# Second layer of a two-layer network: slots find their tokens by an on-chip table instead of a scattered copy

## The reference

```
xn = layernorm(x)
q, k, v = split(xn @ w_qkv);  p = softmax(q k^T / sqrt(128)) per head
attn = (p v) @ w_out
score = relu(xn @ rw1 + rb1) @ rw2 + rb2;  gate = softmax(score over the top 2)
ffn = sum_e gate_e * (relu(xn @ W1[e] + b1[e]) @ W2[e] + b2[e])
x = x + attn + ffn
```

## Time and profile before

| | |
|---|---|
| median of 3 runs | 1158.14 us |
| lowest, highest | 1155.06, 1163.66 us |
| profiled execution | span 1215.3 us, first to last instruction; no other time of it is given |
| mean granted TensorE clock in it | 0.927 of full speed |
| busy in it: PE, DVE, ACT, POOL | 83%, 74%, 65%, 46% |
| weight loads of PE | 45% (beside PE) |

### The profile page before, as it was taken

How to read it: one execution, slowest core, us unless ns; L and a number is a source line. 1 busy time by engine, 2 the same in 40 slices (tenths; PEclk the granted TensorE clock), 3 DMA queues, 4 the chain that set the end, 5 groups by cost and what they waited for, 6 DMA issues and landing times. The chain is left out here.

```text
span 1215.3 us, 24799 instructions
## 1 busy us (share of the span) xinstructions
PE 1012.9 (83%) x9866; PEld 549.0 (45%) x9866; DVE 894.8 (74%) x1046; ACT 790.0 (65%) x851; POOL 563.5 (46%) x569
## 2 busy tenths in 40 slices
PE   6778777889888988888877779986899999998558
PEld 4522222334775333333337776344345656555123
DVE  7888888996648999999959356773685775667137
ACT  3699999998646999999976214311466566554244
POOL 5198887376655588888863005077000000000720
PEclk9799999999699999999997989986799999898679
DMA  8840101120872222222119800002023444321100
GB/s 301 241 160 31 33 33 33 36 69 30 241 159 63 63 72 71 69 70 72 52 43 275 195 2 22 1 25 93 22 79 112 123 124 137 87 79 47 51 25 26
DMA packets 117419, 105.32 MB, mean 87 GB/s; under 512 B 11862, under 2 KB 103666, under 8 KB 116658
## 3 DMA queue, kind: packets, MB, share of 16 engines
q1 hardware_dynamic: 107220, 83.41, 24.1%
q0 software_dynamic: 8512, 20.13, 5.7%
q10 hardware_dynamic: 1571, 0.20, 0.1%
HBM read 62.16 MB, written 38.39 MB: 83 GB/s over the span
## 5 line engine op out<-in xcount | busy, mean ns | idle before, releaser
L261 DVE SCALAR_TENSOR_TENSOR ring<-AD,PT 128x1808 f32<-128x1808 f32 (+15 forms) x128 | 282.9, 2225 | 27.1 <-issue 13.3
L976 PE MATMUL LG<-ring,lred 128*32 128x456 f32 (+15 forms) x2048 | 232.5, 573 | 0.0
L2259 ACT ACTIVATE EX<-SS 128x1024 f32<-128x1024 f32 x128 | 130.8, 1030 | 125.9 <-PE SS L2046 61.8
L2329 DVE TENSOR_REDUCE MX<-SS 128x2 f32<-128x1024 f32 x119 | 144.7, 1219 | 71.1 <-PE SS L2046 52.3
L267 POOL DMA_INDIRECT ys<-rows,goali x80 | 162.2, 2028 | 64.1 <-DVE rows L860 40.5
L916 ACT ACTIVATE ring<-ring 128x3680 f32<-128x3680 f32 (+15 forms) x47 | 161.2, 3430 | 3.6 <-DVE ring L261 3.6
L1001 PE MATMUL SD<-DSf,eyes 99*32 99x456 bf16 (+15 forms) x1280 | 95.2, 374 | 77.6 <-ACT ring L921 66.6
L769 POOL DMA_INDIRECT xs<-rows,sloti x64 | 134.4, 2099 | 30.7 <-issue 19.2
L922 ACT ACTIVATE ring<-ring 128x1824 f32<-128x1824 f32 (+15 forms) x80 | 145.9, 1823 | 0.0
L1963 POOL DMA_INDIRECT XN<-ys,sloti x16 | 16.4, 1024 | 271.7 <-PE SS L2056 267.1
L261 DVE SCALAR_TENSOR_TENSOR ring<-AD,bdmg 128x1808 f32<-128x1808 f32 (+15 forms) x48 | 106.5, 2219 | 0.0
(11 more groups left out here) (419 smaller groups left out, 1767.8 us busy)
## 6 DMA issues: line engine op xcount, KB each, us to landing
w1s<-in_L_ffn_W SPq DMA_DIRECT2D x39, 256.0 KB
w2s<-in_L_ffn_W SPq DMA_DIRECT2D x39, 256.0 KB
band<-ring SPq DMA_DIRECT2D x6, 1024.0 KB, 6.5
xl<-xs SPq DMA_DIRECT2D x20, 272.0 KB, 3.1
xs<-Z SPq DMA_DIRECT2D x5, 1024.0 KB, 8.9
w1s<-w1d SPq DMA_DIRECT2D x80, 64.0 KB
w2s<-w2d SPq DMA_DIRECT2D x80, 64.0 KB
band<-Z SPq DMA_DIRECT2D x4, 1024.0 KB, 9.7
```

The costliest lines, as they stand in the source:

```text
L261: return v.scalar_tensor_tensor(out=tile[:, s, :, t0:T], in0=AD[:, s, :, j + t0:j + T], scalar=extra, in1=AD[:, s, :, PAD + t0:PAD + T], o ...
L976: mm = pe.matmul(LG[32 * b:32 * b + 32, par, s, t0:T], lred[:, s, n % 4, :], ring[:, slot, s, b, t0:T], start=(n % 4 == 0), stop=(n % 4 == 3))
L2259: act.activation(EX[:, Q % 2, hh:hh + 2, t, :], SS[:, slot, :, :], ACT.Exp, scale=SCALE1).then_inc(freed[slot], 1)
L2329: v.tensor_reduce(MX[:, t, p // 2, hh:hh + 2], pairs_of(b, name), AX.X, ALU.max).then_inc(freed[slot], 1)
```

## The change

The array xs goes, with its zeroing and both scatters. XN is stored as it is to xnd in DRAM (one plain DMA of SP). Instead of each pair sending its row to its slot, each slot looks up its token. The table for that is made on chip: DVE compares the pairs' slots with the edges of the 40 tiles (reached_edges, at step 31 of stage 0) and the slots within a tile with the 128 lanes (lanes_of_pairs, four times); POOL makes from the first a mask of pair and tile, and that mask times the token's tile and place (tiles_of_pairs); 32 bf16 products of TensorE (sort_pairs, at step 2 of stage 1) contract both over the pairs into 128 x 120 numbers: for each slot the token's tile, its place, and whether it is a second choice. DVE turns these into row numbers (tokens_of_slots): toki, the token of a slot, and goali, the row of ys for its output. POOL then gathers the rows of xnd for a group of four tiles with four indirect DMAs (gather) and sends the group's outputs with as many indirect scatters to ys (store), where they now stand in the order of the tokens; empty slots go to rows of their own behind. At the end eight plain loads of SP bring them back in place of the 32 gathers. SP's queue keeps the weights, now in a plain loop. The experts start at step 10 of stage 1 instead of 19, and the fillers of steps 3 and 4 there are left out.

The diff, cut to its core:

```diff
@@ -41,8 +41,12 @@
 ROWS = 4 * GROUPS * P
+PAIRS1 = B * T * K1
 AHEAD = 3
-START_STEP = 19
+START_STEP = 10
+SLOT_STEP = 31
+LANE_STEPS = ((0, 32), (0, 33), (0, 35), (1, 0))
+TABLE_STEP = 2
 EPS = 1e-5
@@ -226,8 +230,6 @@
-    xs = nc.dram_tensor("xs", [ROWS, C], F32, kind="Internal").ap()
-    carried[-1].append(xs)
@@ -718,10 +720,6 @@
-                    flat = xs.rearrange("(p n) c -> p (n c)", p=P)
-                    span = GROUPS * 4 * C // 4
-                    for i in range(4):
-                        sp.dma_start(flat[:, span * i:span * i + span], zeros.rearrange("p q t -> p (q t)")[:, 0:span]).then_inc(d_zero, 16)
@@ -927,7 +925,7 @@
-                        act.wait_ge(d_zero, 128)
+                        act.wait_ge(d_zero, 64)
@@ -1453,8 +1451,9 @@
-    attT, wcp, route, b2r, d_zero, (xs,) = carried
-    ys = nc.dram_tensor("ys", [ROWS, C], F32, kind="Internal").ap()
+    attT, wcp, route, b2r, d_zero = carried
+    xnd = nc.dram_tensor("xnd", [B * T, C], F32, kind="Internal").ap()
+    ys = nc.dram_tensor("ys", [PAIRS1 + ROWS, C], F32, kind="Internal").ap()
@@ -1529,6 +1535,8 @@
+            sp.wait_ge(xn_ready, B)
+            sp.dma_start(xnd.rearrange("(n p) c -> p n c", p=P), XN[:]).then_inc(d_w[2], 16)
@@ -1654,6 +1667,12 @@
+    NM = ROWS // P
+    reached = w1s[:].rearrange("p a f -> p (a f)")[:, 0:K1 * TT * (NM + 1)].rearrange("p (n m) -> p n m", m=NM + 1)
+    in_lane = XN[:].rearrange("p t c -> p (t c)").bitcast(BF16).rearrange("p (n r) -> p n r", r=P)
+    in_tile = [buf[:].rearrange("p a n c -> p (a n c)").bitcast(BF16)[:, 0:TT * 3 * NM].rearrange("p (t w m) -> p t w m", t=TT, w=3)
+               for buf in (xl, xsT)]
@@ -1662,6 +1681,7 @@
+    PT1 = PYy[:, 1, 0:3 * NM]
@@ -1824,15 +1845,6 @@
-        def load(n):
-            if n >= 2:
-                sp.wait_ge(ph_ready, bank_use["x", n - 2] + 1)
-            sp.dma_start(xl[:, n % 2, :, :], xs[4 * P * n:4 * P * n + 4 * P, :].rearrange("(n p) c -> p n c", p=P)).then_inc(d_xl[n % 2], 16)
-        def store(n):
-            sp.wait_ge(y_out, n + 1)
-            sp.dma_start(ys[4 * P * n:4 * P * n + 4 * P, :].rearrange("(n p) c -> p n c", p=P), yo[:, n % 2, :, :]).then_inc(d_yo[n % 2], 16)
@@ -1843,20 +1855,17 @@
-        sp.wait_ge(table_ready, 1)
-        for n in range(AHEAD):
+        sp.wait_ge(pairs_dve, 3)
+        sp.wait_ge(pairs_pool, 3)
+        for n in range(TILES):
             weights(n)
-        sp.wait_ge(d_scatter, 16 * TT * K1)
-        load(0)
-        load(1)
-        for kind, n in pieces:
-            if kind == "x" and n + 2 < GROUPS:
-                load(n + 2)
-            if kind == "y":
-                if n + AHEAD < TILES:
-                    weights(n + AHEAD)
-                if n == TILES - 1 or n % 4 == 3:
-                    store(n // 4)
+        filled_by(sp, B - 1, "v")
+        for n in range(2):
+            sp.wait_ge(d_yo[n], 16 * sum(tiles_of[n::2]))
+        for b in range(B):
+            for k in range(K1):
+                at = B * T * k + T * b
+                sp.dma_start(yg[k][:, NT * b:NT * b + NT, :], ys[at:at + T, :].rearrange("(n p) c -> p n c", p=P)).then_inc(d_gather[b], 16)
         for b in range(B - 1):
@@ -1923,12 +1932,37 @@
             link(pool.tensor_tensor(slotf[:, k, :], pick1[:, 1, :, 0], pick1[:, 1, :, 1], ALU.add))
-            link(pool.tensor_copy(sloti[:, k, :], slotf[:, k, :]))
-        def scatter(k):
-            for t in range(TT):
-                pool.indirect_dma_start(xs[:, :], bass.IndirectOffsetOnAxis(ap=sloti[:, k, t:t + 1], axis=0), XN[:, t, :], None,
-                                        bounds_check=ROWS - 1, oob_is_err=True).then_inc(d_scatter, 16)
+        def tiles_of_pairs():
+            pool.wait_ge(pairs_dve, 2)
+            full = [P, TT, NM]
+            here = [in_tile[0][:, :, 1, :], in_tile[1][:, :, 2, :]]
+            for k in range(K1):
+                r = reached[:, TT * k:TT * k + TT, :]
+                last = pool.tensor_tensor(here[k], r[:, :, 0:NM], r[:, :, 1:NM + 1], ALU.subtract)
+            link(last)
+            pool.memset(in_tile[0][:, :, 2, :], 0.0)
+            for k in range(K1):
+                last = pool.tensor_tensor(in_tile[k][:, :, 0, :], here[k], tile_of.unsqueeze(2).to_broadcast(full), ALU.mult)
+            link(last)
+            for k in range(K1):
+                last = pool.tensor_tensor(in_tile[k][:, :, 1, :], here[k], place_of.unsqueeze(2).to_broadcast(full), ALU.mult)
+            last.then_inc(pairs_pool, 1)
+        def gather(n):
+            if n >= 2:
+                pool.wait_ge(ph_ready, bank_use["x", n - 2] + 1)
+            for a in range(4):
+                pool.indirect_dma_start(xl[:, n % 2, a, :], None, xnd[:, :], bass.IndirectOffsetOnAxis(ap=toki[:, 4 * n + a:4 * n + a + 1], axis=0),
+                                        bounds_check=B * T - 1, oob_is_err=True).then_inc(d_xl[n % 2], 16)
+        def store(n):
+            pool.wait_ge(y_out, n + 1)
+            for a in range(tiles_of[n]):
+                pool.indirect_dma_start(ys[:, :], bass.IndirectOffsetOnAxis(ap=goali[:, 4 * n + a:4 * n + a + 1], axis=0), yo[:, n % 2, a, :],
+                                        None, bounds_check=PAIRS1 + ROWS - 1, oob_is_err=True).then_inc(d_yo[n % 2], 16)
@@ -1938,7 +1972,7 @@
-            pool.tensor_scalar(owneri[:], ownerf[:], float(E1 - 1), 0.0, ALU.min, ALU.add).then_inc(table_ready, 1)
+            pool.tensor_scalar(owneri[:], ownerf[:], float(E1 - 1), 0.0, ALU.min, ALU.add).then_inc(pairs_pool, 1)
@@ -1949,19 +1983,19 @@
         slots(0)
-        scatter(0)
         slots(1)
+        pool.sem_inc(pairs_pool, 1)
+        tiles_of_pairs()
         owners()
-        scatter(1)
+        pool.wait_ge(d_w[2], 96)
+        pool.wait_ge(pairs_dve, 5)
+        gather(0)
+        gather(1)
         gate_values()
-        pool.wait_ge(d_scatter, 16 * TT * K1)
-        filled_by(pool, B - 1, "v")
-        for n in range(2):
-            pool.wait_ge(d_yo[n], 16 * ((GROUPS + 1 - n) // 2))
-        for t in range(TT):
-            for k in range(K1):
-                pool.indirect_dma_start(yg[k][:, t, :], None, ys[:, :], bass.IndirectOffsetOnAxis(ap=sloti[:, k, t:t + 1], axis=0),
-                                        bounds_check=ROWS - 1, oob_is_err=True).then_inc(d_gather[t // NT], 16)
+        for n in range(GROUPS):
+            if n + 2 < GROUPS:
+                gather(n + 2)
+            store(n)
@@ -1987,7 +2021,7 @@
-                    pe.wait_ge(d_xl[n % 2], 16 * (n // 2 + 1))
+                    pe.wait_ge(d_xl[n % 2], 64 * (n // 2 + 1))
@@ -1998,6 +2032,16 @@
+        def sort_pairs():
+            pe.wait_ge(pairs_dve, 3)
+            pe.wait_ge(pairs_pool, 2)
+            for k in range(K1):
+                for t in range(TT):
+                    mm = pe.matmul(PT1, in_lane[:, TT * k + t, :], in_tile[k][:, t, :, :].rearrange("p w m -> p (w m)"),
+                                   start=(k == 0 and t == 0), stop=(k == K1 - 1 and t == TT - 1))
+            mm.then_inc(pairs_pe, 1)
@@ -2202,12 +2246,16 @@
                             values(Q, i - 6)
-                        if s == 1 and 1 <= n < START_STEP and (Q == 0 or i >= NT):
+                        if (s, n) == (1, TABLE_STEP + 3):
+                            pe.wait_ge(pairs_dve, 4)
+                        if s == 1 and 1 <= n < START_STEP and n not in (TABLE_STEP + 1, TABLE_STEP + 2) and (Q == 0 or i >= NT):
                             keep_busy(pe, PYy[:, 0, :], ident, 2)
...
                     route(n)
+                if (s, n) == (1, TABLE_STEP):
+                    sort_pairs()
                 if (s, n) == (1, START_STEP):
@@ -2227,7 +2275,7 @@
-                    act.wait_ge(table_ready, 1)
+                    act.wait_ge(pairs_pool, 3)
@@ -2333,7 +2381,38 @@
-            top_k_route(v, link, sc, gate, m8, gt, eq, c0, c1, small, E1, K1, exp_ready, exp_done).then_inc(gate_ready, 1)
+            top_k_route(v, link, sc, gate, m8, gt, eq, c0, c1, small, E1, K1, exp_ready, exp_done).then_inc(pairs_dve, 1)
+        def reached_edges():
+            v.wait_ge(pairs_pool, 1)
+            slot = slotf[:].rearrange("p k t -> p (k t)")
+            full = [P, K1 * TT, NM + 1]
+            link(v.tensor_tensor(reached, slot.unsqueeze(2).to_broadcast(full), edge.unsqueeze(1).to_broadcast(full), ALU.is_ge))
+            v.sem_inc(pairs_dve, 1)
+            link(v.tensor_reduce(tilef, reached[:, :, 1:NM + 1], AX.X, ALU.add))
+            link(v.scalar_tensor_tensor(out=lanef, in0=tilef, scalar=-float(P), in1=slot, op0=ALU.mult, op1=ALU.add))
+            v.wait_ge(d_w[2], 96)
+        def lanes_of_pairs(i):
+            r = slice(8 * i, 8 * i + 8)
+            full = [P, 8, P]
+            ins = v.tensor_tensor(in_lane[:, r, :], lanef[:, r].unsqueeze(2).to_broadcast(full), lane.unsqueeze(1).to_broadcast(full), ALU.is_equal)
+            if i == 3:
+                ins.then_inc(pairs_dve, 1)
```

(20 more changed lines are left out.)

29 lines of the change are left out of this document (21 added, 8 removed).

## The result

The changed kernel takes 1178.8 us (median of 4 runs, 1172.3 to 1182.0), the kernel before on the same chip 1159.55 us: a ratio of **1.0143, interval 1.0095 to 1.019**, so 11 to 22 us slower, with 16.6 us at the ratio itself. (A ratio here is an estimate of its own and differs a little from the quotient of the two medians.) The prediction said 1165 us, within 1129 to 1175.

The account below looks back on a forecast made before the run. Without the late completions, taken as absent from timed runs, a step-by-step ping-pong of TensorE, DVE and ACT bounds the second layer. Terms +5 + 3 + 1 - 2 = +7 us on 1158.1 gave 1165 us, range 1129 to 1175.

Parts of the forecast that it names:

- The stalls: Late TensorE completions in the second layer while POOL issues indirect DMAs in a row: 50 us lost in the profile.
- The choice on which the forecast hung: That the late completions, 50 us, belong to the traced execution and are mostly absent in timed runs.
- rival 1: The stalls are in timed runs too: 50 us go, 5 to 35 return, about 1130 us; chance 0.27.
- DVE at the end of stage 0: New compares and a sum at steps 31 to 35, 7.0 us, of which +5 us reach the path (0 to 8).
- The sort at the seam: 32 TensorE products at step 2 of stage 1, 3.2 us (2.5 to 6), and DVE's work: +3 us.
- The last loads: Eight plain loads replace 32 gathers at the end, saving DVE a wait of 0 to 4 us: -2.
- Experts from step 10: Expert work starting at step 10 of stage 1 instead of 19: +1 us, from -3 to +4.
- The cost: Nine steps of stage 1 go from 1.63 us to 1.82 or 2.52 with expert work: +4 us.
- The return: Ten expert pieces leave steps 26 to 35 of stage 3: some 3 us back, between 1 and 6.
- the signs: Marks of a wrong prediction: median falling about as much as the span, or TensorE waiting at step 2 or 10.
- Rival 2: Tokens miss step 10 of stage 1, TensorE's transposes wait 5 us, sort takes 3 more: 1173 us; chance 0.15.
- Rival 3: The seam costs nothing and stage 3's end gives back 5 us: 1152 to 1158 us; chance 0.1.

Follow-up runs that it names:

- e1: The kernel before again, no edit, traced anew: 1160.8 us, ratio 0.9988.
- e4: The kernel before plus only comparable DVE compares at steps 31, 32, 33 and 35 of stage 0, results unused: 1165.74 us, ratio 1.0037.
- e2: The changed kernel with START_STEP back at 19, all else as changed: 1167.75 us, ratio 1.0069 to the kernel before.
- e13: The kernel before with only the third score bank given up early, at step 10 of stage 1: 1164.31 us, ratio 1.0013.
- e8: The changed kernel with START_STEP at 19 and 32 indirect gathers in place of the eight plain last loads: 1172.5 us, ratio 1.0091.
- e14: The kernel before with START_STEP at 25: 1164.8 us, ratio 1.0015.
- e3: The changed kernel with more filler products behind the scores of steps 33 and 34 of stage 0: 1174.89 us, ratio 1.0128 to the kernel before.
- e5: The changed kernel with four more filler products at each of eight emptied steps of stage 3: 1175.78 us, ratio 1.0108 to the kernel before.
- e6: The changed kernel with no expert pieces at steps 19 to 27 of stage 1: 1180.94 us, ratio 1.0161 to the kernel before.
- e10: e6's edit plus four filler products in each of steps 19 to 27 of stage 1: 1179.28 us, ratio 1.0146 to the kernel before.
- e9: The changed kernel with START_STEP at 19, but the third score bank given up as early as with 10: 1174.88 us, ratio 1.0101.
- e7: The changed kernel with START_STEP at 19 and DVE's table work and the sort moved into stage 1: 1161.48 us, ratio 0.9993.
- e11: As e7, but compare at step 37 of stage 0, sum at step 2 of stage 1, lanes at steps 4 to 7: 1165.93 us, ratio 1.0049.

## Why the prediction was wrong

**The stalls.** The choice on which the forecast hung came out right: the 50 us were not in the timed runs, and rival 1 (1130 us) is out. Their size was nearly right: the last stage of that execution,

```profile
1117.90:1215.26 97.36, 63.02 (x352) 26.75 (x350) 42.46 (x75) 35.32 (x38) 32.72 (x32) 0.79 0.13 36
```

takes 27.2 us more than e1's, its stage 0 (71.8 us) 6.4 more and its seam (36.7 us) 11.3 more, in all 44.9 us. What carried the choice was the comparison of span and median; that tracing makes completions late is not borne out. e1 and the fifteen other kernels were traced as well and have none, so as to its reason the choice was partly luck. The late completions belong to that one execution; what made them is open. The rule that the prediction took from the Trainium skill ("NOTIFIC — the notification-queue block", 7.1 Overflow), that the block which writes trace records backpressures inside itself rather than lose one, pointed to the right one of the two sums, but no run here shows it at work.

**DVE at the end of stage 0, +5 us (0 to 8):** held. e4 measures +4.3 us; in the traces stage 0 is longer than e1's by 3.7 us (e4), 6.8 us (changed kernel) and 4.7 to 6.8 us (the seven other kernels with the same DVE work there).

**The sort at the seam, +3 us (2.5 to 6 for the products):** held. Last maximum to step 9 takes 25.4 us in e1, 27.5 in the changed kernel and e2, so +2.1.

**The last loads, -2 us (0 to -4):** nearer to 0 with START_STEP at 19. I had put DVE's combine one microsecond ahead of the end of the last gather's issue; in e1 it comes four behind it, and waits for nothing. The wait exists in other traces (0.2 us in e4, 0.4 in e13, 2.45 in e8), but in e8 TensorE runs on beside it; only in e14, with START_STEP at 25, is it on the chain.

**Experts from step 10, "+1, from -3 to +4": this is the step that failed.** From e2 to the changed kernel the ratio goes from 1.0069 to 1.0143, some 8.6 us; the two intervals just touch, so it may be anything from nothing to 17. The traces are closer: +5.4 to +7.5 us. The term was a cost of 4 less a return of 3, and both were off. None of the signs came that the prediction had named for being wrong, so only the experiments found this.
- *The cost.* Steps 9 to 29 take 38.0 us in e1, but 45.5 in the changed kernel, 43.4 in e3 and 44.4 in e5: +5.4 to +7.5. Of this 0.6 us fall to the last eleven steps, which the forecast left out. Steps 9 to 18 are near the forecast's +4 only where the clock stays up: 19.8 us at 0.98 (e3) and 19.9 at 0.97 (e6), against 14.9 in e1; at 0.92 they take 20.8 (e5) and 20.7 (e10), and at 0.81 21.9 (changed kernel). The forecast had no term for the clock. I had also read 1.82 and 2.52 us as the price of a step with an expert piece. e9 has no piece at all in steps 9 to 18 and takes 3.9 us more there than e1, e13 4.4 us: START_STEP also sets the banks, and with two of them a step takes 1.82 us without any piece, 0.3 more than with three; the rest of the 3.9 and 4.4 came with a clock of 0.50 in the last steps. In timed runs the bank alone shows 0.1% (e13) to 0.3% (e9 less e2), with intervals that reach to zero, so how the loss of the timed runs divides between bank, pieces and clock stays open.
- *The return.* The end of stage 3 was to give 3 us back. In the traces, step 36 of stage 2 to the end takes 168.7 us (changed kernel) and 173.6 us (e3), and with START_STEP at 19 from 167.4 to 177.1 us, 170.5 on average of eight (e1, e2, e4, e7, e8, e9, e11, e13). No return can be made out, but the scatter is larger than the 3 us looked for. From step 25 to 36 of stage 3 TensorE's busy time fell from 25.37 us (e1) to 18.54 (changed kernel), and the granted clock from 0.82 to 0.72. These steps take 24.3 and 24.9 us without pieces (changed kernel, e3); with pieces 24.9 us in the five of the eight in which the clock is 0.93, and 27.2 to 27.7 in the three in which it is 0.82. The last stage, from there to the end, takes 69.9 and 70.1 us in the two without, 67.5 on average of the eight. In the gap of stage 1, too, a step that lost its piece was no shorter (e6, e10); why is open.

**Sum.** 4.3 for DVE, 2.1 for the sort, 8.6 for the start, 0 for the loads make 15.0 us; measured were 16.6 (11 to 22). The 8.6 is itself the difference between the changed kernel and e2, so this tests only the other terms: 6.4 us against the 8.0 (5.0 to 11.0) that e2 loses. e7, which has the start back at 19 and the table out of stage 0, is level with the kernel before: these two edits together are the loss.

**The rivals.** Rival 2 came near the time (1173 us) but not by its mechanism: the tokens were there at step 10. Its doubling of POOL's operations beside DVE was seen in two of six, 2.2 us in place of 1.25, and moved nothing. The Trainium skill's rule on the shared interfaces ("GPSIMD Engine Reference", 1 Specifications) agrees with these two, which ran beside compares with two inputs. Rival 3, the free seam, is out by e2 and e4.

## What to carry to other kernels

A constant that starts one piece of work earlier may end another resource's use: look up every place where it stands (here the pieces, the third bank and the fillers of stage 1), and price each by itself. Read a step's pace from a whole run of like steps, not from one pair, at the clock that the stretch will have, and don't book a return where work leaves a stretch until the trace shows that this work sets the stretch's length. Where a profiled execution is far from the timed ones, take a second trace before the argument is built on it.

## What the runs showed of the hardware

- One execution of the kernel before had completions of TensorE arriving late while POOL issued indirect DMAs in a row; the three stretches concerned took 44.9 us more than in e1. (Of the longest wait, 28.5 us, ACT has 18.0 us in e1 as well.) e1, e4, e13 and e14, with the same 64 DMAs, had none.
- The granted clock of the same stretch differs from execution to execution. In e14 the last maximum of stage 0 to step 9 took 21.0 us at 1.00, in e1 25.4 us at 0.65. That is over 4 of the 20 us over which the 114 runs of the kernel before spread.
- A stretch with less work for TensorE ran at a lower clock: steps 18 to 29 at 0.72 with TensorE busy 19.50 us (e6), at 1.00 with 21.44 (e1) and 23.42 (e10); steps 9 to 18 with two banks and no pieces at 0.78 (e9) and 0.74 (e13), with pieces at 0.81 (changed kernel) to 0.98 (e3). In e13 TensorE was busy 6.80 of the 9.12 us at 1.00 that came before the fall to 0.50.
